# A fused four-layer graph network: the back transpose at the head of a step, reciprocals spread by GpSimd, one tile of each additive pair copied by ScalarE

## The reference, cut to what matters

```python
# layer 1: four heads, then a fifth attention on their projection ("GAT2")
h = einsum('bnc,hdc->bhnd', x, Wh)
attn = softmax(where(mask, h @ h.T, NEG)); out_h = attn @ h + bh      # per head
h2 = leaky_relu(cat(out_h)) @ Wo; out2 = softmax(where(mask, h2 @ h2.T, NEG)) @ h2 + bo
# layers 2 and 3: additive attention
e = leaky(left[:, :, None] + right[:, None, :]); out = softmax(where(mask, e, NEG)) @ Xw
# after each: x = layernorm(x + out)
```

## Time and profile before

| | us |
|---|---|
| median of 3 runs | 5605.79 (5604.51 to 5607.32) |
| the profiled execution | 5605.99 |
| its span on the chip | 5604.2 |
| PE, DVE, ACT, POOL busy | 5262.9, 4332.8, 3770.6, 623.4 |

### The profile page before, as it was taken

How to read it: one execution, slowest core, us unless ns; L and a number is a source line. 1 busy time by engine, 2 the same in 40 slices (tenths; PEclk the granted TensorE clock), 3 DMA queues, 4 the chain that set the end, 5 groups by cost and what they waited for, 6 DMA issues and landing times.

```text
span 5604.2 us, 130791 instructions
## 1 busy us (share of the span) xinstructions
PE 5262.9 (94%) x52866; PEld 4507.4 (80%) x52866; DVE 4332.8 (77%) x7321; ACT 3770.6 (67%) x5617; POOL 623.4 (11%) x956
## 2 busy tenths in 40 slices
PE   8499999999999999999999999999999999999866
PEld 6388888888888888888888888888888888888755
DVE  5677678778787787878787787877878787887766
ACT  3266567776686766767677766867667676777566
POOL 4400010000200011000110002000110001100111
PEclk9699999999999999999999999999999999999988
DMA  5200000000000000000000000000000000000000
GB/s 180 62 16 11 18 9 9 9 15 11 13 13 5 15 15 13 13 3 18 17 9 9 11 12 15 13 5 15 15 13 13 3 18 15 9 9 5 13 1 5
DMA packets 135478, 94.28 MB, mean 17 GB/s; under 512 B 93792, under 2 KB 112864, under 8 KB 134880
## 3 DMA queue, kind: packets, MB, share of 16 engines
q1 hardware_dynamic: 134880, 85.92, 6.1%
HBM read 35.03 MB, written 8.91 MB: 8 GB/s over the span
## 4 chain that ended last, share of the span: by engine, by line
PE 76%; DVE 8%; ACT 6%; issue 5%; DVEq 1%; POOLq 0%; DMA 0%; SPq 0%; POOL 0%; ACTq 0%
PE po L1099 25%; PE ring L1072 25%; PE pss L1063 10%; PE pss L1064 10%; DVE rows L1374 3%; DVE pt L1386 3%; ACT rows L1278 2%; PE ring L1021 2%; ACT pss L1259 2%; PE ring L1087 2%; DVEq L312 1%; PE ring L1038 1%; ACT pt L1223 1%; PE ring L1031 1%; PE ring L1002 1%
## 5 line engine op out<-in xcount | busy, mean ns | idle before, releaser
L1072 PE MATMUL ring<-ident,rows 128*128 128x128 f32 x14336 | 1935.5, 277 | 111.3 <-DVE pt L1386 70.8
L1278 ACT ACTIVATE rows<-rows,nm 128x2048 f32<-128x2048 f32 x896 | 1795.0, 2003 | 344.4 <-DVE nm L1374 338.9
L1386 DVE COPY pt<-ring 128x512 f32<-128x512 f32 x2048 | 1331.4, 686 | 872.8 <-PE ring L1072 865.9
L1072 PEld LDWEIGHTS ring<-ident,rows 128*128 128x128 f32 x14336 | 1595.6, 141 | 354.2 <-issue 163.9
L1099 PE MATMUL po<-pt,hn 128*64 128x128 f32 x28672 | 1777.9, 277 | 42.0 <-ACT ot L1234 21.9
L1099 PEld LDWEIGHTS po<-pt,hn 128*64 128x64 f32 x28672 | 1563.8, 138 | 195.8 <-issue 175.9
L1223 ACT COPY pt<-ring 128x512 f32<-128x512 f32 x1536 | 837.2, 588 | 696.1 <-PE ring L1072 685.3
L1374 DVE CUSTOM_DVE_ANT_0 rows<-pss,mask,nm 128x1024 f32<-128x1024 f32 x896 | 1150.0, 1284 | 120.1 <-issue 2.0
L1374 DVE CUSTOM_DVE_ANT_0 rows<-pss,mask 128x1024 f32<-128x1024 f32 x896 | 1078.6, 1204 | 73.8 <-PE pss L1064 16.4
L1063 PE MATMUL pss<-ha 128*128 128x512 f32 x2560 | 1062.7, 415 | 14.0 <-DMA ha<-hb 12.7
L1064 PE MATMUL pss<-ha,hb 128*128 128x512 f32 x2560 | 1009.7, 394 | 0.0
(11 more groups left out here) (104 smaller groups left out, 2732.9 us busy)
## 6 DMA issues: line engine op xcount, KB each, us to landing
hb<-ha SPq DMA_DIRECT2D x160, 128.0 KB, 2.3
ha<-hb SPq DMA_DIRECT2D x160, 128.0 KB, 2.3
adjb<-in_adj SPq DMA_DIRECT2D x32, 512.0 KB, 5.4
xb<-in_x SPq DMA_DIRECT2D x16, 256.0 KB, 2.9
x<-t SPq DMA_DIRECT2D x16, 256.0 KB, 2.4
xin<-x SPq DMA_DIRECT2D x32, 128.0 KB, 2.5
xb<-x SPq DMA_DIRECT2D x8, 512.0 KB, 3.9
out<-xb SPq DMA_DIRECT2D x32, 128.0 KB, 1.9
```

The source lines that it names most:

```text
L1072: last = nc.tensor.transpose(tile[:, r * P:(r + 1) * P], rows[:, row.slot, jb * P:(jb + 1) * P], ident[:])
L1278: nc.scalar.activation(rows[:, row.slot, :], rows[:, row.slot, :], ACT.Exp, scale=-1.0, bias=nm[:, row.place, 1:2], accum_out=rs[:, row.pl ...
L1386: nc.vector.tensor_copy(pt[:, CH * q:CH * (q + 1), row.k % SLOTS, :], tile_of("turn", row.k, q)[:].rearrange("p (j n) -> p j n", n=P)).the ...
```

## The change

The back transpose and its copy move from the middle of a step to its head: on PE behind the scores and ahead of the tasks, on ACT ahead of everything. In `uses()` it now stands at the head too, held 1500 instead of 2600. DVE writes only the 128 x 2 reciprocals for all rows, and GpSimd spreads them for head rows (`widen`, at the step after DVE's), with a semaphore of its own, for which the back transpose waits. In the first row of each additive pair ACT copies tile 1 too, which DVE did. In the first six turns the second half of GAT2's projection and its two followers move two steps later (102, 103, 104 to 104, 105, 106).

```diff
@@ class Segment
-                    by_dve = q >= 2 if row.gat else q >= 1
+                    by_dve = q >= 2 if row.gat or not row.odd else q >= 1
@@ uses()
             yield None, (1900 if row and row.gat else 0), 0
+            if self.back(s):
+                yield ("back", self.back(s).pair), 150, 1500
...
-            if self.back(s):
-                yield ("back", self.back(s).pair), 150, 2600
@@ main_loop
+    low = last + (9 if last_turn else 11)
-    tasks += [(last + 9, "proj", GAT2, 1), (last + 10, "low", GAT2, 1), (last + 11, "hn", GAT2, 1)]
+    tasks += [(low, "proj", GAT2, 1), (low + 1, "low", GAT2, 1), (low + 2, "hn", GAT2, 1)]
@@ GpSimd
+            def widen(row):
+                if row.unit >= H:
+                    return
+                scales = rc[:, row.place - 1:row.place + 1].unsqueeze(2).to_broadcast([P, 2, D])
+                if row.pair or back_c.n:
+                    wait(back_c, back_c.n + row.pair)
+                wait(rc_c, rc_c.n + row.pair + 1)
+                nc.gpsimd.tensor_copy(rcw[:].rearrange("p (r n) -> p r n", r=2), scales).then_inc(rcw_ready, 1)
...
                 for s in segment.steps:
+                    if segment.odd(s - 5):
+                        widen(segment.odd(s - 5))
                     if segment.finished(s):
                         finish(segment.finished(s))
@@ PE turn_back
-                    wait(rc_c, rc_c.n + row.pair + 1)
+                    rcw_c.n += 1
+                    wait(rcw_c)
@@ PE run_segment
                         dot_products(row)
+                    if segment.back(s):
+                        turn_back(segment.back(s))
...
-                    if segment.back(s):
-                        turn_back(segment.back(s))
@@ ACT run_segment
+                    if segment.back(s):
+                        take_back(segment.back(s))
                     for task in segment.tasks.get(s, ()):
                         run_task(*task)
...
-                    if segment.back(s):
-                        take_back(segment.back(s))
@@ DVE invert_sums
-                if row.unit >= H:
-                    nc.vector.reciprocal(rc[:, pair], rs[:, pair]).then_inc(rc_ready, 1)
-                    return
-                if row.pair or back_c.n:
-                    wait(back_c, back_c.n + row.pair)
-                nc.vector.reciprocal(rcw[:].rearrange("p (r n) -> p r n", r=2),
-                                     rs[:, pair].unsqueeze(2).to_broadcast([P, 2, D])).then_inc(rc_ready, 1)
+                nc.vector.reciprocal(rc[:, pair], rs[:, pair]).then_inc(rc_ready, 1)
```

More of the change, by code:

```diff
@@ L765, in attention_layers @@
         rc_ready = sem("rc_ready")
+        rcw_ready = sem("rcw_ready")
         out_done = sem("out_done")
@@ L880, in _ @@
             rc_c = Count(rc_ready)
+            back_c = Count(back_ready)
             def wait(count, n=None):
@@ L938, in run_segment @@
                 copied_c.n += segment.pairs
+                back_c.n += segment.pairs
                 rc_c.n += segment.pairs
@@ L960, in _ @@
             z_c = Count(z_ready)
-            rc_c = Count(rc_ready)
+            rcw_c = Count(rcw_ready)
             freed, where, used = [None] * BANKS, [None], [None]
@@ L1131, in run_segment @@
                 exp_c.n += segment.blocks
-                rc_c.n += segment.pairs
                 ot_c.n += segment.pairs
@@ L1310, in _ @@
             exp_c = Count(exp_ready)
-            back_c = Count(back_ready)
             where = [None]
@@ L1417, in run_segment @@
                 out_c.n += segment.pairs
-                back_c.n += segment.pairs
                 exp_c.n += segment.blocks
```

## The result

The change takes the median from 5605.79 to **5538.88 us** (5535.12 to 5544.85), a ratio of 0.9885 with the interval [0.9868, 0.9903]: 67 us, or 1.2%, faster. The forecast was 14 us and its range ended at 5575. The direction was right and the size was not. Of all executions reported here one, of `a_again`, ran at a lower granted clock throughout (0.905, 5714.36 us); it is set aside.

A forecast was written before the change was run, and what follows sets the result against it. TensorE, busy 94%, was taken as the bound, with only idle time to win. Six turns -11, last turn +0.8, prologue -0.85 and epilogue -3 gave -14 us on 5606.0: 5592 us, range 5575 to 5613.

The forecast's parts named there:

- VectorE's relief: Shorter reciprocals, 202 us off VectorE, and 128 fewer tile copies hide nothing TensorE waits for in a turn.
- Only its 20 us of idle time can be won: In a 654.75 us turn TensorE is busy 634.84, so only its 20 us of idle time can be won.
- The projection's own term: Steps 102 to 106: moving GAT2's projection two steps later saves 2.7 us a turn, a cautious sum of 3.0.
- The epilogue, -3: Lone additive pairs: -0.17 each in ADD2, +0.15 in ADD1, -0.3 with layer norm; with three doubled banks, -3 us.
- Second additive rows, +4.4: At 16 steps a turn, tiles behind the back transpose wait for a bank: +4.4 us a turn.
- `hn` and `xn` heads, -1.4: Head of additive steps: `hn` transposes no longer get the bank just made; with the projection at 94, -1.4 us a turn.
- Last turn, +0.8: The last turn has neither the moved projection nor `xn`: +0.8 us.
- Rival 3: Second additive rows: VectorE copies sooner, so no bank wait; 5565 us; chance 0.17 together with rival 4.
- Rival 2: ScalarE becomes the bound in lone additive rows and ends later in mixed steps; 5635 us, half of it 5613; chance 0.13.
- rival 4: First additive rows: the chain is loose, 0.3 us at 8 x 7 steps; 5575 us; chance 0.17 together with rival 3.
- rival 1: Half the gains do not arrive; the moved projection's 16 us shrink to 5; 5603 us, no change; chance 0.25.
- three signs of being wrong: Second-row waits above 0.8 us, TensorE waiting for `rcw`, or steps 102 to 106 falling by less than 1 us.

The follow-up runs named there:

- a_again: The kernel after, run once more unchanged to learn the scatter: 5538.35 us, 0.988 of the kernel before.
- a_backmid: Kernel after with the back transpose and its copy in the middle of the step again: 5544.34 us, 0.9891.
- m_best: Kernel after with the back transpose in the middle only where the step's row is additive and the row turned is dot-product, head elsewhere: 5494.28 us, 0.9806.
- b_spread: Kernel before with only the reciprocals changed, VectorE writing 128 x 2 and GpSimd spreading them: 5576.93 us, 0.9953.
- b_tile: Kernel before with only tile 1 of the first additive rows copied by ScalarE: 5596.69 us, 0.9987.
- a_oldproj: Kernel after with GAT2's second projection back at its old place, steps 102 to 104, in all turns: 5557.23 us, 0.9914.
- b_proj: Kernel before with only GAT2's second projection two steps later in six turns: 5575.23 us, 0.9949.
- b_fill: Kernel before with 14 unneeded transposes of the identity in the wait at step 102: 5587.98 us, 0.997.
- a_recdve: Kernel after with the reciprocals spread by VectorE as before, `widen` gone: 5553.9 us, 0.991.

## Why the prediction was wrong, point by point

The terms of the sum came out near their sizes. What failed are two steps ahead of it: VectorE's relief was put at nothing in the turns, from the reading of one step, and is worth 18 to 19 us there; and TensorE's clock, some 13 us there, had no term. The epilogue's handovers, left out as well, add nearly 7.

- **"VectorE's relief ... hides nothing that TensorE waits for": wrong, and the first large miss.** Alone it is worth 28 us, in the kernel after 15. With the clock taken out it is 18 to 19 us in the six turns, where the sum had 0. The step read for it, 32, is indeed closed by TensorE, but was taken for all. At step 41 the wait carries ScalarE's name, and ScalarE's lift was itself late by VectorE. The trace had said so, in rows that were not read: ScalarE's lifts waited 54.8 us for `nm` (19.7 with this edit alone), and its exponentials 338.9 us (439 times), its second largest wait (285.1 with this edit alone, 184.5 after).
- **"Only its 20 us of idle time can be won": wrong.** Busy time held waits too short to show as idle time, and the clock. Of the 52 us won in the six turns 15 were idle time, about 13 clock, and some 24 the short waits.
- **The clock: no term at all in the sum.** Busy time was taken as fixed. The 5.38 us of the earlier trace rows were taken as the price of the projection, from one turn, and its 3.71 in the next turn was not looked up. It is worth some 13 us in the turns and part of the epilogue's gain, and makes -2.7 at steps 101 to 106 into -4.9. The projection's own term was right: 16 us for six turns, 15 and 18 with the clock taken out. Of the clock, only what stood at step 102 follows from the change; that step 88 fell less often is luck as far as the runs show.
- **The epilogue, -3: mis-sized, -11 measured.** The terms for the pairs held. The handovers between layers, where the back transpose is on the only path, were not in the sum; they bring 3.1 and 3.6 us, half of the second in clock. `a_backmid` has the old length, and `m_best` the new one.
- **Second additive rows, +4.4: right as a difference from before** (+4.5 in the turn, +4.4 as an average of six). The first such row, 0.49 forecast, was 0.49; step 83, +1.2, was +1.5. Beside the other edits the move costs more there, 8.2 us (`a_backmid`), because the relief that it hides is then worth something; the forecast, which gave the relief nothing, could not see this.
- **Doubled banks, first rows, GpSimd's bounds: right.** -2.2 for -1.7; -0.1 for -0.3. The copy takes 290 ns, between the two ends, and TensorE never waits for it. That GpSimd does not slow the score pass was right, but for a wrong reason: the pass at 2199.49 ran 1.16 us because it stood behind the long reciprocal (last section), and not for want of a lock.
- **`hn` and `xn` heads, -1.4: direction right, size half** (-2.9). `a_backmid` has none of it, so it belongs to the head place and its deal of the banks. What makes it twice the forecast was not separated.
- **Last turn, +0.8: wrong, -3.8.** It too gains from the relief and the clock: alone, the spread takes 5 us off it. Its time at half clock fell from 20.5 to 13.7 us, at most 3.4 us of the gain. How much is from each was not measured.
- **The rivals.** None of them was it. Rival 3 had the right side and the wrong mechanism: the wait in the second rows is there. Rival 2's ScalarE bound did not show, rival 4's chain of the first rows did not give (-0.1 for -0.3), and rival 1's moved projection kept its gain.
- **The signs.** Of the three signs of being wrong one appeared, and narrowly: at step 83 a tile waited 0.84 us for the `ob` copy, over the bound of 0.8, in a step for which the sum itself had +1.2. The other waits and the pairs of the epilogue came as foretold, and the copy was shorter than 0.4 us. What gave it away was the turn: 646 us for 653. The signs tested the terms that were in the sum, and what was missing was not among them.

## What to carry to other kernels

Follow each wait one engine further than its name: what the named engine waited for just before is the path. TensorE's busy time can hold waits and a slow clock, so it is no bound on what can be won. Compare the same instructions' busy time at two places, since a short wait in a dense stream of matmuls may cost as much again behind it, in clock; filling it with work that nobody needs is a cheap trial. And where a step is moved, read the places where nothing follows it as well as the loop that fills most of the time.

## What the runs showed of the hardware

- Waits of 1.6 to 2.5 us in an otherwise busy stream were followed by 3.4 us at 1.2 GHz in 11 of 12 places of the kernel before and 3 of 6 of the kernel after. The length of the wait does not decide it. At step 102, behind 2.1 to 2.4 us, the clock fell in 5 of 6 turns of before, 4 of `b_spread`, 4 of `b_tile` and 2 of `a_oldproj`; at step 88, behind a wait of 2.0 us (1.64 in some turns), in 6 of before, 5 of `b_tile`, 4 of `b_spread`, 3 of `b_proj`, 2 of `b_fill` and none of `a_backmid`. What decides was not settled. These are counts of one profiled execution each.
- VectorE's first score pass takes 1220 ns in the kernel after and 1204 with the spread taken back; the second pass keeps its 1284. Groups by shape, after and `a_recdve`:

```profile
L1389 DVE CUSTOM_DVE_ANT_0 rows<-pss,mask 128x1024 f32<-128x1024 f32 x896 | 1093.3, 1220 | 80.8 <-PE pss L1080 18.0
```

```profile
L1378 DVE CUSTOM_DVE_ANT_0 rows<-pss,mask 128x1024 f32<-128x1024 f32 x896 | 1078.9, 1204 | 71.6 <-PE pss L1068 13.7 <-ACT pss L1263 10.9 <-issue 3.8
```

  It looks as if GpSimd's copies slowed VectorE, and they do not. In the kernel after, the 253 passes that overlap such a copy take 1217 ns in the mean, the 643 others 1222. The difference is in `a_recdve`, and likewise in before: the 246 passes right behind the long reciprocal take 1161 ns, the other 650 take 1220 (step 41 above: 1.16 us behind the 0.94 of the reciprocal, 1.20 with the short one). Why a pass is 60 ns shorter there stays open. The warning in the Trainium skill ("Perfetto Trace Analysis", Optimizing Scalar/DVE Operations), that moving work between the two might not help, does not come true here: VectorE is rid of 202 us of reciprocals, and no pass is slower for the copies beside it.
